# Cross-attention with image tokens: the products with the values, one step for both query tiles

## The chip, the cores and the metric

One core of a Trainium2 chip. The metric is device time in microseconds. The kernel before takes 710.52 us, the median of 3 runs (709.02 to 711.61).

## The reference

All in float32: x is 2 x 2048 x 640, the context 2 x 154 x 1024, of which the last 8 tokens are image tokens (4 "dummy", 4 for boxes). 20 heads of 32.

```python
q = split_heads(x @ w_q)
k, v = split_heads(text @ w_k), split_heads(text @ w_v)            # 146 text tokens
out_text = merge(softmax(q @ k.T / sqrt(32)) @ v)
k_ip, v_ip = split_heads(ip @ w_k_ip), split_heads(ip @ w_v_ip)    # 8 image tokens
out_ip = merge(softmax(q @ k_ip.T / sqrt(32) + mask_of_boxes) @ v_ip)
out = (out_text + out_ip) @ w_out + b_out + x
```

## The kernel before, in words

**Blocks.** The 4096 queries are done in 16 blocks of 256, each of two tiles of 128 (`qt` 0 and 1). Heads are taken in 5 groups `g` of 4. One loop iteration works on three blocks: the attention of block t - 1 ("back"), the query projection and first maxima of block t ("front"), and the transposed input of t + 1 ("next"). Four tables write down the order on each engine by hand: `STEPS` (TensorE), `ACT_STEPS` (ScalarE), `DVE_STEPS` (VectorE), `POOL_STEPS` (GpSimd); `SP_STEPS` holds the order of SyncE's DMAs.

**Steps.** X: transpose the input. Q g: project a group's queries in 15 matmuls (L1046); ScalarE copies the rounded part, VectorE writes the rest (L816). S g, qt, pair: scores of two heads (L1104); VectorE takes the maxima (L824, L825). AUX: the maxima, transposed, become rows of the stacked queries `q_stack`. ST g, u: transposed scores minus maxima; u = 0 and 1 are 128 text keys of two heads each (L1129), u = 2 the tail: 18 text keys and 8 image keys of all four heads at 32 rows for each head (L1134). ScalarE takes exp twice for u < 2, to 16 bits (`p_hi`) and in place (L676, L678), VectorE writes the difference `p_lo` (L852); for u = 2 ScalarE writes `p_tail`, 128 rows of float32 (L680). PV g, qt: the product with the values. AT: transpose the result; O: project it (L1046).

**PV before.** One step for each query tile, into one PSUM bank. First the tail, a float32 matmul over 128 rows and 264 columns, which the trace shows as two passes (L1150): 8 pieces of 33 columns, 4 heads' text part and 4 heads' image part with their denominators. Then 12 matmuls in 16 bits for the four heads' main keys (L1156, L1158, L1159). VectorE inverts the 8 denominators (L860) and multiplies them in (L865, L868) into `o_parts`; GpSimd adds three parts into `attn` (L530, L535).

**Banks.** X, Q, AUX, PV and O share three "general" PSUM banks in turn, S has two, ST has three. A step waits until the bank's user three places before has been read:

```python
    def user_before(self, gen):
        mine, theirs = users(self.stages), users(self.earlier)
        n = gen - GENERAL_BANKS
```

**Waits used below.** PV g waits for `exp_done` and `p_split` of its group. ST waits for `p_lo` three ST steps before. S waits for the maxima two S steps before (`s_freed`). AT waits for `att_done`. SyncE's step STK 0 rewrites `q_stack` for groups 0 to 2 of the next block: it waits for ST of those groups, the last of which is ST 2, 1, issues 12 copies and one of the mask, and S 0, 0, 0 waits for all of them (`stack_in`).

**Set-up.** The weights of keys and values are loaded in pieces; keys are copied into `k_stack` by 24 DMAs; the values are made in 8 units between the first steps (`V_PLACES`).

Of the kernel before, what the change touches and what calls it, by code (L numbers as in the profile page):

```python
# [31 lines left out]
F32 = mybir.dt.float32  # L32
# [3 lines left out]
ALU = mybir.AluOpType  # L36
# [3 lines left out]
P = 128  # L40
# [48 lines left out]
    (FRONT, "S", 2, 0, 0), (FRONT, "S", 2, 0, 1), (BACK, "O", 1, 0), (NEXT, "X", 2), (FRONT, "S", 2, 1, 0),  # L89
    (FRONT, "S", 2, 1, 1), (BACK, "O", 1, 1),  # L90
# [41 lines left out]
V_UNITS = [("ip", 0), ("ip", 1), ("text", 0), ("text", 1),  # L132
           ("main", 0, 0, 512), ("main", 0, 512, D), ("main", 1, 0, 512), ("main", 1, 512, D)]
V_TAILS = 4
V_BANKS = (5, 6, 7, 5, 6, 7, 5, 6)
V_PLACES = {
# [4 lines left out]
}  # L141
V_COPY_PLACES = {(0, "S", 0, 0, 0): (0, 1), (0, "S", 0, 0, 1): (2, 3), (1, "Q", 0): (4,), (1, "Q", 1): (5,), (1, "ST", 0, 2): (6, 7)}
V_SPLIT_PLACES = {(1, "S", 3, 0, 0): (4,), (1, "S", 3, 1, 0): (5,), (1, "S", 4, 0, 1): (6, 7)}
W_O_HIGH = {("Q", 0): (0, 1), ("Q", 1): (2, 3, 4)}
W_O_LOW = {("S", 3, 0, 1): (0, 1), ("S", 3, 1, 1): (2, 3), ("S", 4, 0, 0): (4,)}


GENERAL = {"X": 1, "Q": 1, "AUX": 1, "PV": 1, "O": 1}
# [17 lines left out]
def users(stages):  # L166

    return [s for s in STEPS if s[0] in stages and s[1] in GENERAL]

# [59 lines left out]
def attention_kernel(nc, x, ctx, boxes, wq, wk, wv, wk_ip, wv_ip, wo, b_out,  # L229
# [5 lines left out]
    with ExitStack() as stack:  # L235
# [20 lines left out]
        v_tail = [sb(f"v_tail{b}", [P, GROUPS, 8 * VW]) for b in range(BATCHES)]  # L256
# [29 lines left out]
        inv_den = sb("inv_den", [P, QT, 8])  # L286
# [8 lines left out]
        o_parts = sb("o_parts", [P, QT, 12, DH])  # L295
# [17 lines left out]
        product_2 = [general[i][:, 0:4 * VB].rearrange("p (e d) -> p e d", d=VB)[:, :, VW:VB] for i in range(GENERAL_BANKS)]  # L313
# [7 lines left out]
        s_wv, s_wv_ip, s_wq, s_wo, s_wk_ip = sem("wv_in"), sem("wv_ip_in"), sem("wq_in"), sem("wo_in"), sem("wk_ip_in")  # L321
# [6 lines left out]
        s_kst = [sem(f"k_stack{b}_in") for b in range(BATCHES)]  # L328
        s_vp, s_vc, s_ktail = sem("v_product"), sem("v_copied"), sem("k_tail_ready")
# [11 lines left out]
        norm_first = sem("first_part_normalised")  # L341
# [22 lines left out]
        def split_turn(n):  # L364

            return n - V_TAILS

# [3 lines left out]
        def keys_to_stack(queue, b, parts):  # L371

            for row, src in parts:
                for j in range(4):
                    queue.dma_start(k_stack[b][row:row + DH, j:HEADS:4, :].bitcast(F32),
                                    src[DH * j:DH * (j + 1), :, b, :].bitcast(F32)).then_inc(s_kst[b], 16)
# [13 lines left out]
        def _(sp):  # L390
# [300 lines left out]
        def _(dve):  # L691
# [111 lines left out]
            def body(it):  # L803
# [4 lines left out]
                for stage, kind, args, gen, sc in it.steps(DVE_STEPS):  # L808
# [437 lines left out]
```

## Time and profile before

| | |
|---|---|
| median of 3 runs | 710.52 us |
| profiled execution | 708.68 us |
| its span | 706.9 us |
| TensorE busy | 676.1 us, 96% |
| VectorE busy | 534.9 us, 76% |
| ScalarE busy | 290.4 us, 41% |
| GpSimd busy | 209.2 us, 30% |
| TensorE's mean granted clock | 0.995 of full speed |

The span goes from the first to the last instruction; 1.78 us lie around it. Blocks in the middle repeat every 38.4 us. Matmul records overlap: one starts before the one ahead has drained, so a matmul's cost in a stream is the distance between starts, and the chain of waits shows just that. On VectorE too the next instruction starts somewhat before the end that is shown.

### The profile page before, as it was taken

The numbers are of one execution on the slowest core, as the hardware profiler recorded it, in microseconds if no ns is written. First come the engines' busy times: TensorE is split into PE (matmuls) and PEld (weight loads), VectorE is DVE, ScalarE is ACT, GpSimd is POOL, SyncE is SP. The second block draws the span as 40 slices with busy tenths as digits, with TensorE's granted clock in tenths as the row PEclk, the third lists the DMA queues.
The fourth block names the chain that finished last, engine by engine and source line by source line (L and its number), as shares of the span: only waits on it lengthen the run. The fifth ranks groups of instructions, "written<-read, shape, count | busy, mean of one in ns | idle before, by whom it ended". The sixth has DMA issues, their size and how long they took to land.

```text
span 706.9 us, 19241 instructions
## 1 busy us (share of the span) xinstructions
PE 676.1 (96%) x6570; PEld 623.6 (88%) x6570; DVE 534.9 (76%) x1689; ACT 290.4 (41%) x636; POOL 209.2 (30%) x359
## 2 busy tenths in 40 slices
PE   6996988999999999999999999999999999999976
PEld 5794677989999999999998999999999989899866
DVE  4432678787878788887979787888879797879774
ACT  1232253351727263544526171726344352617161
POOL 5200006042423314150514242231515041423333
PEclk9998999999999999999999999999999999999999
DMA  9999326443526253534444352625354443434220
GB/s 295 379 278 210 93 36 139 131 106 86 146 71 177 68 157 93 132 97 130 102 118 118 90 154 69 177 73 150 89 136 100 129 103 110 122 89 124 68 76 38
DMA packets 74208, 89.40 MB, mean 126 GB/s; under 512 B 9440, under 2 KB 58080, under 8 KB 74156
## 3 DMA queue, kind: packets, MB, share of 16 engines
q1 hardware_dynamic: 70800, 86.48, 46.0%
q10 hardware_dynamic: 3372, 2.45, 1.8%
q8 instruction: 22, 0.36, 0.2%
q14 instruction: 14, 0.11, 0.1%
HBM read 39.21 MB, written 10.62 MB: 70 GB/s over the span
## 4 chain that ended last, share of the span: by engine, by line
PE 84%; DMA 6%; SPq 5%; DVE 4%; issue 1%; ACT 0%; POOL 0%; DVEq 0%
PE psum L1046 38%; PE psum L1104 10%; PE psum L1150 9%; PE psum L1134 5%; PE psum L1129 5%; SPq L384 3%; PE psum L1158 3%; DMA q_stack<-mask_scratch 3%; PE psum L1006 3%; DMA wo_raw<-in_L_xattn_w_k_ip 2%; PE psum L1159 2%; PE psum L918 2%; PE psum L1173 2%; PE psum L980 2%; PE psum L1156 1%
## 5 line engine op out<-in xcount | busy, mean ns | idle before, releaser
L530 POOL TENSOR_TENSOR attn<-o_parts 128x128 f32<-128x128 f32 x160 | 73.3, 458 | 421.9 <-DVE o_parts L865 387.3
L824 DVE TENSOR_REDUCE neg_max<-psum 128x2 f32<-128x292 f32 x320 | 144.8, 453 | 58.7 <-PE psum L1104 58.1
L1046 PE MATMUL psum<-wo_both,at_hi 128*128 128x320 f32 x640 | 153.2, 313 | 0.0
L1104 PE MATMUL psum<-k_stack,q_stack 104*128 104x154 f32 x640 | 114.5, 288 | 8.7 <-DMA q_stack<-mask_scratch 6.6
L1046 PE MATMUL psum<-xt_hi,wq_hi 128*128 128x256 f32 x400 | 114.1, 285 | 0.1
L1046 PE MATMUL psum<-xt_hi,wq_lo 128*128 128x256 f32 x400 | 111.1, 278 | 0.0
L1046 PE MATMUL psum<-xt_lo,wq_hi 128*128 128x256 f32 x400 | 111.1, 278 | 0.0
L852 DVE TENSOR_TENSOR p_lo<-psum,p_hi 128x512 f16<-128x512 f32 x160 | 107.9, 682 | 2.5 <-ACT psum L678 2.5
L1046 PEld LDWEIGHTS psum<-wo_both,at_hi 128*128 128x128 f32 x640 | 109.6, 188 | 0.0
L676 ACT ACTIVATE p_hi<-psum 128x512 f16<-128x512 f32 x160 | 95.2, 595 | 31.0 <-PE psum L1129 31.0
L1104 PEld LDWEIGHTS psum<-k_stack,q_stack 104*128 104x128 f32 x640 | 90.0, 191 | 19.6 <-issue 10.2
L1150 PE MATMUL psum<-v_tail,p_tail 128*128 128x264 f32 x320 | 101.5, 398 | 2.9 <-DVE o_parts L868 1.6
L1046 PE MATMUL psum<-wo_both,at_lo 128*128 128x320 f32 x320 | 98.7, 308 | 0.0
L678 ACT ACTIVATE psum<-psum 128x512 f32<-128x512 f32 x160 | 96.6, 603 | 0.0
L663 ACT ACTIVATE q_hi<-psum 128x256 fp32r<-128x256 f32 x80 | 30.9, 387 | 133.0 <-PE psum L1046 130.5
L535 POOL TENSOR_TENSOR attn<-attn,o_parts 128x128 f32<-128x128 f32 x160 | 73.2, 457 | 12.6
L1046 PEld LDWEIGHTS psum<-xt_hi,wq_hi 128*128 128x128 f32 x400 | 75.4, 189 | 0.3 <-DVE q_lo L816 0.3
L1046 PEld LDWEIGHTS psum<-xt_hi,wq_lo 128*128 128x128 f32 x400 | 75.4, 188 | 0.1
L1046 PEld LDWEIGHTS psum<-xt_lo,wq_hi 128*128 128x128 f32 x400 | 75.2, 188 | 0.0
L865 DVE TENSOR_TENSOR o_parts<-psum,inv_den 128x256 f32<-128x256 f32 x160 | 67.9, 424 | 8.6 <-POOL attn L535 3.1
L1158 PEld LDWEIGHTS psum<-v_main,p_hi 128*128 128x128 f16 x640 | 56.4, 96 | 20.1
L1159 PE MATMUL psum<-v_main,p_lo 128*128 128x65 bf16 x640 | 71.6, 191 | 0.0
(95 smaller groups left out, 1249.1 us busy)
## 6 DMA issues: line engine op xcount, KB each, us to landing
q_stack<-q_hi SPq DMA_DIRECT2D x128, 96.0 KB
x_in<-in_x SPq DMA_DIRECT2D x16, 640.0 KB, 5.4
x_res<-in_x SPq DMA_DIRECT2D x16, 640.0 KB, 5.4
out<-out_sb SPq DMA_DIRECT2D x32, 320.0 KB
q_stack<-q_hi SPq DMA_DIRECT2D x128, 64.0 KB
q_stack<-q_lo SPq DMA_DIRECT2D x60, 96.0 KB
q_stack<-q_lo SPq DMA_DIRECT2D x60, 64.0 KB
q_stack<-aux_a SPq DMA_DIRECT2D x48, 64.0 KB, 2.4
```

The lines of the kernel that those rows point to most:

```text
L530: nc.gpsimd.tensor_tensor(cols, o_parts[:, qt, 0:4, :], o_parts[:, qt, 4:8, :], ALU.add).then_inc(att_half, 1)
L535: nc.gpsimd.tensor_tensor(cols, cols, o_parts[:, qt, 8:12, :], ALU.add).then_inc(att_done, 1)
L676: nc.scalar.activation(p_hi[:, -g % P_SLOTS, 2 * u:2 * u + 2, :].rearrange("p h q -> p (h q)"), src[:], ACT.Exp)
L678: nc.scalar.activation(src[:], src[:], ACT.Exp).then_inc(exp_done, 1)
L824: nc.vector.tensor_reduce(dst[:, :, 0], src[:, :, 0:TEXT], AX_X, ALU.max, negate=True)
L852: nc.vector.tensor_tensor(p_lo[:, -g % P_SLOTS, 2 * u:2 * u + 2, :], scores_t[ST_TURN[(g, u)] % ST_BANKS][:].rearrange("p (h q) -> p h q", ...
L865: nc.vector.tensor_tensor(o_parts[:, qt, 0:8, :], product_1[it.general_bank(gen)][:, :, 0:DH], inv_den[:, qt, :].unsqueeze(2).to_broadcast ...
L1046: last = nc.tensor.matmul(ps, l(c), r(c), start=(i == 0), stop=(i == len(terms) - 1))
L1104: last = nc.tensor.matmul(scores[sc % 2][:, i * CTX:(i + 1) * CTX], q_stack[0:ROW_MAX, h, P * qt:P * (qt + 1)], k_stack[batch][0:ROW_MAX, ...
L1150: nc.tensor.matmul(product_1[it.general_bank(gen)][:, 0:8, :], p_tail[:, -g % P_SLOTS, queries], v_tail[batch][:, g, :].rearrange("p (e d) ...
L1158: nc.tensor.matmul(bank_a[:, VB * j:VB * (j + 1)], hi, values[:, 0:VB], start=False, stop=False)
L1159: last = nc.tensor.matmul(bank_a[:, VB * j:VB * (j + 1)], lo, values[:, 0:VB], start=False, stop=(j == 3))
```

## The change

PV becomes one step a group, for both query tiles. Its tail product is cut by rows: rows 0 to 63 (heads 0 and 1 of the group) go into one general bank, rows 64 to 127 (heads 2 and 3) into the next, 132 columns each, the two query tiles side by side in a bank. The main products follow, first those of bank r = 0, then of r = 1. VectorE normalises each bank by itself, GpSimd adds both query tiles in one instruction. PV 4, 1, which stood after AT 0, 1, goes with PV 4, 0. Waits are made to fit.

```diff
-    (BACK, "ST", 1, 0), (FRONT, "Q", 2), (BACK, "AUX", 1), (BACK, "ST", 2, 2), (BACK, "ST", 1, 1), (BACK, "PV", 0, 0),
-    (BACK, "ST", 2, 0), (BACK, "ST", 2, 1), (BACK, "PV", 0, 1), (FRONT, "Q", 3), (BACK, "ST", 3, 0),
-    (BACK, "PV", 1, 0), (BACK, "ST", 3, 2), (BACK, "ST", 3, 1), (BACK, "PV", 1, 1), (BACK, "PV", 2, 0),
-    (BACK, "PV", 2, 1), (BACK, "ST", 4, 0), (BACK, "ST", 4, 1), (BACK, "PV", 3, 0), (BACK, "PV", 3, 1),
-    (BACK, "ST", 4, 2), (FRONT, "Q", 4), (BACK, "PV", 4, 0), (FRONT, "S", 0, 0, 0), (BACK, "AT", 0, 0),
-    (FRONT, "S", 0, 0, 1), (NEXT, "X", 0), (FRONT, "S", 0, 1, 0), (FRONT, "S", 0, 1, 1), (BACK, "AT", 0, 1),
-    (BACK, "PV", 4, 1), (FRONT, "S", 1, 0, 0), (BACK, "AT", 1, 0), (NEXT, "X", 1), (FRONT, "S", 1, 0, 1),
-    (BACK, "O", 0, 0), (BACK, "AT", 1, 1), (FRONT, "S", 1, 1, 0), (FRONT, "S", 1, 1, 1), (BACK, "O", 0, 1),
...
+    (BACK, "ST", 1, 0), (FRONT, "Q", 2), (BACK, "AUX", 1), (BACK, "ST", 2, 2), (BACK, "ST", 1, 1), (BACK, "PV", 0),
+    (BACK, "ST", 2, 0), (BACK, "ST", 2, 1), (FRONT, "Q", 3), (BACK, "ST", 3, 0), (BACK, "PV", 1), (BACK, "ST", 3, 2),
+    (BACK, "ST", 3, 1), (BACK, "PV", 2), (BACK, "ST", 4, 0), (BACK, "ST", 4, 1), (BACK, "PV", 3), (BACK, "ST", 4, 2),
+    (FRONT, "Q", 4), (BACK, "PV", 4), (FRONT, "S", 0, 0, 0), (BACK, "AT", 0, 0), (FRONT, "S", 0, 0, 1),
+    (NEXT, "X", 0), (FRONT, "S", 0, 1, 0), (FRONT, "S", 0, 1, 1), (BACK, "AT", 0, 1), (FRONT, "S", 1, 0, 0),
+    (BACK, "AT", 1, 0), (NEXT, "X", 1), (FRONT, "S", 1, 0, 1), (BACK, "O", 0, 0), (BACK, "AT", 1, 1),
...
 DVE_STEPS = [
...
+    (BACK, "ST", 1, 0), (FRONT, "Q", 2), (BACK, "ST", 1, 1), (BACK, "PV", 0), (BACK, "ST", 2, 0), (BACK, "ST", 2, 1),
+    (FRONT, "Q", 3), (BACK, "PV", 1), (BACK, "ST", 3, 0), (BACK, "ST", 3, 1), (BACK, "PV", 2), (BACK, "ST", 4, 0),
+    (BACK, "ST", 4, 1), (BACK, "PV", 3), (FRONT, "Q", 4), (BACK, "PV", 4), (FRONT, "S", 0, 0, 0),
+    (FRONT, "S", 0, 0, 1), (BACK, "AT", 0, 0), (NEXT, "X", 0), (FRONT, "S", 0, 1, 0), (FRONT, "S", 0, 1, 1),
+    (BACK, "AT", 0, 1), (FRONT, "S", 1, 0, 0), (BACK, "AT", 1, 0), (FRONT, "S", 1, 0, 1), (NEXT, "X", 1),
...
 SP_STEPS = [
-    (BACK, "AUX", 0), (BACK, "LAST"), (NEXT, "XIN"), (BACK, "XRES"), (BACK, "AUX", 1), (FRONT, "STK", 0), (FRONT, "STK", 1),
-    (BACK, "STORE"),
+    (NEXT, "XIN"), (BACK, "AUX", 0), (BACK, "LAST"), (BACK, "XRES"), (BACK, "AUX", 1), (FRONT, "STK", 0),
+    (FRONT, "STK", 1), (BACK, "STORE"),
...
-GENERAL = {"X": 1, "Q": 1, "AUX": 1, "PV": 1, "O": 1}
+GENERAL = {"X": 1, "Q": 1, "AUX": 1, "PV": 2, "O": 1}
...
+                        tiles = [it.general_bank(gen + r) for r in range(2)]
+                        for r in range(2):
+                            free_general(it, gen + r)
+                        for qt in range(QT):
+                            queries = slice(P * qt, P * (qt + 1))
+                            for r in range(2):
+
+                                rows = slice(64 * r, 64 * (r + 1))
+                                nc.tensor.matmul(product_1[tiles[r]][:, 4 * qt:4 * qt + 4, :], p_tail[rows, -g % P_SLOTS, queries],
+                                                 v_tail[batch][rows, g, :].rearrange("p (e d) -> p e d", d=VW),
+                                                 start=(qt == 0), stop=False)
+                        for r in range(2):
+                            for qt in range(QT):
...
+                            last.then_inc(pv_ready, 1)
...
+                        for r in range(2):
+                            part, first = o_parts[:, g % 2, r, :, :], product_1[it.general_bank(gen + r)]
+
+                            dve.wait_ge(pv_ready, 2 * n + r + 1)
+                            nc.vector.reciprocal(inv_den[:, r, :], first[:, :, DH]).then_inc(recip_done, 1)
+                            dve.wait_ge(recip_done, 2 * n + r + 1)
+                            nc.vector.tensor_tensor(part[:, 0:8, :], first[:, :, 0:DH],
+                                                    inv_den[:, r, :].unsqueeze(2).to_broadcast([P, 8, DH]), ALU.mult)
...
-                        pe.wait_ge(att_done, t * 10 - 10 + (7 if u == 0 else 9) + qt)
+                        pe.wait_ge(att_done, t * 5 - 5 + (4 if u == 0 else 5))
```

The set-up changes too. Of the three pieces of the values' weights (L407), SyncE loads the second and third only after the first STK 0. Of the 8 key copies that SyncE issued ahead of STK 0, 4 go to GpSimd, as do 8 that ScalarE issued for the second batch. The main value units are cut at 256 columns instead of 512, and two of them stand ahead of the text tails, which so move behind the first scores.

```diff
-                    keys_to_stack(sp, 0, K_PARTS[:2])
+                    keys_to_stack(sp, 0, K_PARTS[:1], s_kst[0])
...
+                        if not it.back and n == 0:
+                            load_values(1)
+                            load_values(2)
...
+            keys_to_stack(nc.gpsimd, 0, K_PARTS[1:2], s_kst_own[0])
+            pool.wait_ge(q_freed, GROUPS)
+            keys_to_stack(nc.gpsimd, 1, K_PARTS[:2], s_kst_own[1])
```

## Rows read from the trace of the kernel before

**Rows 1.** The page, part 1: busy time, share of the span, instructions.

```profile
PE 676.1 (96%) x6570; PEld 623.6 (88%) x6570; DVE 534.9 (76%) x1689; ACT 290.4 (41%) x636; POOL 209.2 (30%) x359
```

**Rows 2.** Windows: stretch, then busy time of each engine, granted clock, DMA share, GB/s.

```profile
313.68:352.07 38.39, 38.34 (x381) 36.29 (x380) 31.70 (x103) 16.94 (x39) 12.02 (x21) 1.00 0.43 115
331.00:348.00 17.00, 17.00 (x209) 15.55 (x207) 15.20 (x46) 11.74 (x26) 7.27 (x16) 1.00 0.52 135
```

**Rows 3.** Chain of waits, 331 to 353 us: start, length, who.

```profile
333.93 0.45 PE psum L1150 x2
...
334.72 0.55 PE psum L1129 x4
...
338.89 0.55 PE psum L1134 x4
...
340.48 0.53 PE psum L1150 x2
...
344.97 1.77 PE psum L1046 x15
...
347.56 0.22 DVE inv_den L860
...
348.80 0.09 DVE neg_max L825
...
350.74 0.26 PE psum L1104 x2
...
352.07 1.07 PE psum L1046 x7
```

**Rows 4.** Groups by line: busy us, mean ns | idle before, releaser.

```profile
L1150 PE MATMUL psum<-v_tail,p_tail 128*128 128x264 f32 x320 | 101.5, 398 | 2.9 <-DVE o_parts L868 1.6 <-ACT p_tail L680 0.9 <-DVE p_lo L852 0.4
...
L1150 PEld LDWEIGHTS psum<-v_tail,p_tail 128*128 128x128 f32 x320 | 49.1, 191 | 3.3 <-DVE o_parts L868 1.7 <-ACT p_tail L680 1.0 <-issue 0.6
...
L1012 PE MATMUL psum<-w_kv,rest_t 128*26 128x160 f32 x128 | 5.0, 300 | 1.4 <-issue 1.4
...
L530 POOL TENSOR_TENSOR attn<-o_parts 128x128 f32<-128x128 f32 x160 | 73.3, 458 | 421.9 <-DVE o_parts L865 387.3 <-DMA bias<-in_L_xattn_b_out 34.6
```

**Rows 5.** Chain of waits, 136 to 162 us.

```profile
137.18 0.41 PE psum L1104 x4
...
152.20 3.29 DMA q_stack<-mask_scratch
```

**Rows 6.** VectorE's timeline, 314 to 353 us: start, length, line, tiles.

```profile
334.19 0.40 DVE L816 TENSOR_TENSOR q_lo<-psum,q_hi 128x256 fp32r<-128x256 f32 x1
...
341.30 0.68 DVE L852 TENSOR_TENSOR p_lo<-psum,p_hi 128x512 f16<-128x512 f32 x1
341.89 0.20 DVE L860 RECIPROCAL inv_den<-psum 128x8 f32<-128x8 f32 x1
...
342.66 0.20 DVE L860 RECIPROCAL inv_den<-psum 128x8 f32<-128x8 f32 x1
...
349.25 0.68 DVE L876 TENSOR_TENSOR at_lo<-psum,at_hi 128x512 fp32r<-128x512 f32 x1
349.84 0.45 DVE L824 TENSOR_REDUCE neg_max<-psum 128x2 f32<-128x292 f32 x1
...
350.29 0.68 DVE L754 TENSOR_TENSOR xt_lo<-psum,xt_hi 128x512 fp32r<-128x512 f32 x1
```

**Rows 7.** ScalarE's timeline, 334 to 336 us.

```profile
334.01 0.59 ACT L676 ACTIVATE p_hi<-psum 128x512 f16<-128x512 f32 x1
334.49 0.61 ACT L678 ACTIVATE psum<-psum 128x512 f32<-128x512 f32 x1
```

**Rows 8.** SyncE's DMA issues, 314 to 362 us.

```profile
335.30 2.52 SPq L384 DMA_DIRECT2D q_stack<-q_hi  x4
...
343.18 0.34 SPq L458 DMA_DIRECT2D q_stack<-mask_scratch  x1
```

**Rows 9.** Chain of waits, 0 to 128 us: the first scores wait for this.

```profile
51.36 11.06 DMA q_stack<-mask_scratch
```

More of the change, by code:

```diff
@@ L166, in users @@
 def users(stages):
-    return [s for s in STEPS if s[0] in stages and s[1] in GENERAL]
+    return [(*s, r) if GENERAL[s[1]] > 1 else s
+            for s in STEPS if s[0] in stages and s[1] in GENERAL for r in range(GENERAL[s[1]])]
 class Iteration:
@@ L255, in attention_kernel @@
         v_main = [sb(f"v_main{b}", [P, HEADS, VALUES], BF16) for b in range(BATCHES)]
-        v_tail = [sb(f"v_tail{b}", [P, GROUPS, 8 * VW]) for b in range(BATCHES)]
+        v_tail = [sb(f"v_tail{b}", [P, GROUPS, 4 * VW]) for b in range(BATCHES)]
         max_cols = [80, 16 * len(SET_B)]
@@ L294, in attention_kernel @@
             ctx_t = sb("ctx_t", [P, CC, BATCHES * TEXT], where=setup)
-        o_parts = sb("o_parts", [P, QT, 12, DH])
+        o_parts = sb("o_parts", [P, 2, 2, 12, DH])
         attn = sb("attn", [P, QT, D])
@@ L312, in attention_kernel @@
                      for i in range(GENERAL_BANKS)]
-        product_2 = [general[i][:, 0:4 * VB].rearrange("p (e d) -> p e d", d=VB)[:, :, VW:VB] for i in range(GENERAL_BANKS)]
+        product_2 = [psum[:, 512 * i:512 * i + 8 * VB].rearrange("p (q e d) -> p q e d", q=QT, d=VB)[:, :, 0:2, VW:VB]
+                     for i in range(GENERAL_BANKS)]
         s_ident, s_ctx, s_ctx_rest = sem("ident_in"), [sem(f"ctx{b}_in") for b in range(BATCHES)], sem("ctx_rest_in")
@@ L328, in attention_kernel @@
         s_kst = [sem(f"k_stack{b}_in") for b in range(BATCHES)]
+        s_kst_own = [sem(f"k_stack{b}_in_by_gpsimd") for b in range(BATCHES)]
         s_vp, s_vc, s_ktail = sem("v_product"), sem("v_copied"), sem("k_tail_ready")
@@ L645, in body @@
                             w_high(GROUPS + n)
-                    if not it.back and (kind, *args) == ("S", 0, 0, 1):
-                        act.wait_ge(stored, 16 * BATCHES)
-                        keys_to_stack(act, 1, K_PARTS[:2])
                     if kind == "X":
@@ L992, in make_values @@
                     if (n, first) == (2, 0):
-                        pe.wait_ge(s_wv, 16 * len(W_V_PIECES))
-                    if first == 0 and 3 <= n < 7:
-                        pe.wait_ge(s_vc, n - 2)
-                    if (n, first) == (7, 0):
-                        pe.wait_ge(s_vsplit, V_PARTS * split_turn(4) + 1)
+                        pe.wait_ge(s_wv[0], 16)
+                    if (n, first) == (4, 0):
+                        pe.wait_ge(s_wv[1], 16)
+                        pe.wait_ge(s_wv[2], 16)
+                    before = [m for m in range(n) if V_BANKS[m] == V_BANKS[n]]
+                    if first == 0 and before:
+                        if before[-1] in V_MAIN:
+                            pe.wait_ge(s_vsplit, V_PARTS * split_turn(before[-1]) + 1)
+                        else:
+                            pe.wait_ge(s_vc, before[-1] + 1)
                     ps = v_bank(n)
@@ L1161, in body @@
-                        last.then_inc(pv_ready, 1)
+                        g, = args
+                        if isinstance(t, int) and t == 1 and g == 0:
+                            pe.wait_ge(s_vc, 5)
+                            pe.wait_ge(s_vsplit, 3 * V_PARTS)
+                        pe.wait_ge(exp_done, t * ST_ALL - ST_ALL + 1 + max(ST_TURN[(g, u)] for u in range(3)))
+                        pe.wait_ge(p_split, t * 10 - 10 + 2 * g + 2)
+                        tiles = [it.general_bank(gen + r) for r in range(2)]
@@ new lines, in body @@
+                        for r in range(2):
+                            for qt in range(QT):
+                                queries = slice(P * qt, P * (qt + 1))
+                                for i in range(2):
+                                    j = 2 * r + i
+                                    at = VB * (4 * qt + i)
+                                    values, ps = v_main[batch][:, 4 * g + j, :], general[tiles[r]]
+                                    lo, hi = (p[:, -g % P_SLOTS, j, queries] for p in (p_lo, p_hi))
+                                    nc.tensor.matmul(ps[:, at + VW:at + VB], hi, values[:, VB:VALUES], start=False, stop=False)
+                                    nc.tensor.matmul(ps[:, at:at + VB], hi, values[:, 0:VB], start=False, stop=False)
+                                    last = nc.tensor.matmul(ps[:, at:at + VB], lo, values[:, 0:VB],
+                                                            start=False, stop=((qt, i) == (QT - 1, 1)))
+                            last.then_inc(pv_ready, 1)
```

158 lines of the change are left out of this document (71 added, 87 removed), and 9 rows, old and new, of the table V_PLACES.

## The prediction

> **What bounds the kernel now.** The page comes first: TensorE is busy for 96% of the span, VectorE for 76% [rows 1]. That alone would say that each microsecond taken from TensorE is gained, so the windows come next, one for a block and one for its PV stretch. A block in the middle takes 38.39 us; TensorE is busy throughout, VectorE for 31.70. But from 331 to 348 us, where ST and PV stand, VectorE has 15.20 us of work in 17.00 [rows 2]. The share of 76% is an average over two unlike halves, and the change takes time from TensorE in the half where VectorE is nearly full. The chain of waits shows how near: PV 4, 0 ends at 347.54, then the chain goes over VectorE (normalisation, then maxima) and comes back to TensorE only at 348.89, where S 0, 1, 0 needs a score bank [rows 3]. The reader is to see that VectorE already ends a wait once a block.
>
> **What TensorE saves.** In the chain a tail product costs 0.45 us behind an ST step and 0.53 behind another PV [rows 3]; there are seven of the first and three of the second in a block: 3.15 + 1.59 = 4.74 us. The 12 matmuls behind each take 0.34 (333.93 + 0.45 to 334.72), and their number stays. The new tail has four products of 64 rows and 132 columns a group. A pass of 264 columns takes 0.45 / 2 = 0.22, one of 132 so 0.11. No row shows two halves by rows. The bounds: if the halves run side by side, weight loads too, four passes, 0.44, and the start that PV behind PV shows, 0.53 - 0.45 = 0.08: 0.52. If nothing overlaps, eight passes, 0.88, and 0.08: 0.96. The nearest row is that of four tiles by columns, L1012: 128 records take 5.0 us, 0.039 each, where a pass of 160 columns alone would take 0.22 x 160 / 264 = 0.13 [rows 4]. Tiles do run side by side, so I take 0.55. Gain: 4.74 - 5 x 0.55 = 2.0 us a block. What could spoil it is the weights: S, with 154 columns, takes 0.41 / 4 = 0.10 a matmul [rows 5], more than its columns need (0.55 / 4 = 0.14 for 256, so 0.08), thus a load costs about 0.10, and eight one after the other 0.8. That is a rival below.
>
> The Trainium skill speaks against the change here: "TensorE: Matmul & The Clock Gate", section "LDWEIGHTS (loading the stationary operand)", says that a load takes as long for 32 rows as for 128, since the columns count, and "TensorEngine Tiling (Array Packing)", section "Key Properties", that a change of the tiling mode drains the engine, but also that tiles load and multiply independently. By the first with loads in line the tail would stay near 0.9 and the gain be nil; by the last it would be what I take. No run here shows which holds for rows.
>
> **What the new order makes wait.** VectorE's work per block stays: a bank's normalisation costs 0.77 (341.89 to 342.66) as before, ten of them; p_lo 0.59, AT 0.59, maxima 0.45 [rows 6], X, of AT's shape, 0.59. What changes is which bank is free when. I go through one block in the chain's times, with the new orders. ScalarE needs 1.10 from the start of p_hi to the end of the second exp [rows 7].
>
> 1. PV 0 takes two general banks at once. The second is that of Q 2, which VectorE frees at 334.19 + 0.40 = 334.59 [rows 6]. TensorE is there at 333.93 [rows 3]; before, only PV 0, 1 needed that bank, after two ST steps. Stall 0.70. Behind it stand ST 2, 0 and 2, 1, and behind them ScalarE and SyncE's STK 0.
> 2. PV 0: 334.63 to 335.86 (0.55 + 2 x 0.34). VectorE, now told to do ST 1, 1 first, idles until its exp ends at 335.10 and does it to 335.75; banks 0 and 1 to 337.3.
> 3. ST 2, 0 and 2, 1 end at 336.41, Q 3 (1.77) 338.18, ST 3, 0 338.42, PV 1 339.65. VectorE, waiting for the exps, does p_lo of group 2 to 338.9, Q 3 to 339.3, PV 1 from 339.33 (bank 0 ready) to 340.89, ST 3, 0 to 341.5, ST 3, 1 (exp ends 341.6) to 342.24.
> 4. ST 3, 2 (0.55) and 3, 1 end at 340.44, PV 2 341.67, ST 4, 0 and 4, 1 342.22. PV 3 needs the first bank of PV 2, which VectorE gets to after ST 3, 1: 342.24 + 0.78 = 343.02. Stall 0.84.
> 5. PV 3 ends at 344.29, ST 4, 2 344.85, Q 4 346.62, PV 4 347.87. VectorE is busy to 346.56, waits for Q 4, and normalises PV 4 from 347.55 to 349.11.
> 6. Then maxima of S 0, 0, 0 and 0, 0, 1, AT, X, maxima of S 0, 1, 0: 349.11 + 0.45 + 0.45 + 0.59 + 0.59 + 0.45 = 351.64. S 1, 0, 0 needs that last bank. Before, PV 4, 1 stood in front of S 1, 0, 0 and its normalisation behind the maxima, so that S 1, 0, 0 started at 350.74 [rows 3]. From there to O 0, 0 TensorE takes 352.07 - 350.74 = 1.33, now too: O 0, 0 starts at 351.68 + 1.33 = 353.0.
>
> Before it started at 352.07. From O 0, 0 on to the next PV 0 nothing is changed and VectorE has its idle time, so the block takes 0.94 us more: 2.0 saved, some 2.9 more in stalls. After each stall a weight load stands open, 0.08; two of the stalls are new, so I say 1.1 us a block.
>
> GpSimd's adds go from 128 to 256 elements; one of 128 takes 458 ns [rows 4], two of 256 at most 4 x 0.46 = 1.8 us, so PV 4 is in `attn` by 351.0, and AT 0, 1 behind it lies before S 1, 0, 0 is free (351.68): nothing. STK 0 costs nothing either, but just so: SyncE starts at 335.30, right after ST 2, 1, and issues the mask's copy at 343.18, 7.9 later [rows 8]; such a copy landed 3.29 after its issue [rows 5]. ST 2, 1 now ends at 336.41, S 0, 0, 0 can start at 336.41 + 7.9 + 3.3 + 0.1 = 347.7, and TensorE comes at 347.87. XIN ahead of AUX 0 on SyncE is cheap: its buffer is free before, and both issue long before ST.
>
> **Set-up and end.** The first scores wait for the mask's copy, issued at 51.36 and 11.06 us under way [rows 9], behind all other transfers. With fewer copies and two weight pieces less ahead of it I give it 5 us back; the text tails (L1012, 5.0 us [rows 4]), which filled that wait, then stand in TensorE's way later. Net -1, between -5 and +3. In the last block, where only "back" runs, PV 4 with both tiles stands before AT 0, 1: +1.
>
> **The sum**, against the profiled execution: 708.7 + 15 x 1.1 + 1 - 1 = 725. The median of before is 1.8 above that execution (0.3%), so I forecast 726 for the median.
>
> **Rivals.**
> - *Weight loads in line* (20%). The halves share one way for weights, the tail costs up to 0.95. The same steps with 0.95 give: PV 2's first bank free at 343.8, PV 3 to 345.5, PV 4 normalised at 350.67, 1.56 later, thus 2.65 a block: 708.7 + 15 x 2.65 + 2 = 750. For it: loads of 0.10. Against: four column tiles at 0.039 a record.
> - *Faster: VectorE's waits for exps close up* (18%). In my steps VectorE idles 1.8 us between 334.59 and 349.11, mostly waiting for ScalarE. If it finds work there, PV 4 is normalised by 348.0 and TensorE's 2.0 us come through until STK 0 holds it: S 0, 0, 0 at 347.73, O 0, 0 at 347.73 + (352.07 - 347.54 - 0.79 of PV 4, 1) = 351.5, 0.6 a block less: 708.7 - 15 x 0.6 - 2 = 698. It decides where PV 4's second bank is normalised less than 14.3 us after TensorE reached PV 0, and not 15.2. Against: the order is fixed, and each exp follows an ST that itself stands behind PV.
> - *No change* (7%): both effects meet, within 0.3% (2.1 us), which is about what a measurement of this kernel can tell.
> - My forecast (55%): 713 to 738 by itself, from the stalls being 0.7 us a block smaller or larger and the set-up's 4.
>
> Faster has 0.18, same 0.07, slower 0.75. The range reaches from 700, near the faster case, to 752, past the loads in line; outside lies some 15%.
>
> **What would show it.** Right: the PV stretch's tail at about 0.55 a group in the chain; TensorE's L1150 waiting on VectorE (q_lo L816 at PV 0, o_parts at PV 3) 15 times each; S 1, 0, 0 waiting on the maxima; the block at 39.5 us, with TensorE's busy time some 2 us lower and VectorE's 31.7 unchanged. Wrong: a block under 38.4 with VectorE full from PV 0 to O 0, 0; a tail of 0.9; or idle time at S 0, 0, 0 that the mask's copy ends.

## The result

The changed kernel takes 749.56 us, the median of 4 runs (744.59 to 751.46), beside 710.44 for the kernel before on the same chip: 1.0536 of its time, 95% interval [1.0505, 1.0566]. The forecast was 726. So the direction was right, and the loss, 39 us, is two and a half times the 15.5 that I gave it. The profiled execution's span is 748.2 us. Some executions of a kernel are over 1.5% above its fastest, at a lower granted clock: the medians here hold them, the ratios leave them out.

Part 1 of the page, after, beside [rows 1]:

```profile
span 748.2 us, 19481 instructions
...
PE 682.3 (91%) x6890; PEld 629.3 (84%) x6890; DVE 537.1 (72%) x1689; ACT 290.5 (39%) x636; POOL 185.7 (25%) x211
```

TensorE is busy for 6 us more in all, in a span that is 41 us longer. The windows show one block in the middle, from one O 0, 0 to the next, and its ST and PV stretch, as in [rows 2]:

```profile
245.47:286.37 40.90, 38.07 (x400) 35.87 (x400) 31.85 (x102) 16.95 (x39) 10.17 (x12) 1.00 0.44 108
262.92:280.00 17.08, 15.64 (x212) 14.23 (x210) 14.58 (x44) 11.74 (x26) 5.13 (x8) 1.00 0.50 119
```

A block takes 40.90 us where it took 38.39. From the first O 0, 0 to the fifteenth the two traces move apart by 34.9 us, 2.49 in each of 14 steps; 1.5 us lie ahead of the first and 4.9 behind the fifteenth, 41.3 in all. VectorE's work is 31.85, as said. TensorE idles for 2.83, and is busy for 0.27 less than before. I had forecast nearly the same idle time (2.9) and 2.0 less work. Where it idles, the groups by line tell (busy, mean ns | idle before, releaser):

```profile
L1131 PE MATMUL psum<-k_stack,q_stack 104*128 104x154 f32 x640 | 114.6, 290 | 21.8 <-DVE neg_max L842 15.3 <-DMA q_stack<-mask_scratch 6.4
...
L1181 PE MATMUL psum<-v_tail,p_tail 64*128 64x132 f32 x640 | 58.6, 302 | 24.0 <-DVE o_parts L887 12.6 <-DVE q_lo L833 11.1 <-ACT p_tail L697 0.3
```

L1181 is the tail product: 11.1 / 15 = 0.74 a block for q_lo at PV 0 (forecast 0.70), 12.6 / 15 = 0.84 for o_parts at PV 3 (forecast 0.84). L1131 is S, with 15.3 / 15 = 1.0 a block for the maxima, about half of it at S 0, 1, 0 and half at S 1, 0, 0. A fifth piece, 0.35 us at AT 0, 1 for GpSimd's `attn`, had been put at nothing; it costs nothing, since the chain does not pass through it. The chain of waits of the same block, beside [rows 3] (L1193 to L1195 are the main products, L1161 ST's tail, L1070 is Q and O):

```profile
266.16 0.41 DVE q_lo L833
...
266.62 0.72 PE psum L1181 x8
267.34 0.12 PE psum L1193
...
268.13 0.56 PE psum L1156 x4
268.69 1.77 PE psum L1070 x15
270.46 0.24 PE psum L1156 x2
270.70 0.65 PE psum L1181 x8
271.35 0.12 PE psum L1193
...
272.14 0.57 PE psum L1161 x4
...
275.65 0.72 PE psum L1181 x8
...
279.48 0.65 PE psum L1181 x8
...
284.34 0.37 DVE neg_max L841
...
284.85 0.45 PE psum L1131 x2
...
286.37 2.24 PE psum L1070 x15
```

Every wait of the forecast is there, at its place. What is not there is a PV of 0.55 + 0.68 = 1.23 us: they take 1.44 behind an ST step (270.70 to 272.14) and 1.51 after a wait (266.62 to 268.13). Less 0.68 for the 24 main products the tail costs 0.76 and 0.83. Laid on each other at ST 1, 1, in front of PV 0, the two traces are 68.03 us apart. With that shift the prediction's ledger reads:

| | forecast | measured | late by |
|---|---|---|---|
| PV 0 starts | 266.60 | 266.62 | 0.02 |
| PV 1 starts | 270.39 | 270.70 | 0.31 |
| PV 3 starts, behind o_parts | 275.03 | 275.65 | 0.62 |
| PV 4 starts | 278.61 | 279.48 | 0.87 |
| PV 4 normalised | 281.08 | 282.25 | 1.17 |
| S 1, 0, 0 starts, behind the maxima | 283.65 | 284.85 | 1.20 |
| O 0, 0 starts | 284.97 | 286.37 | 1.40 |

It gets later by 0.25 to 0.31 from row to row down to PV 4's normalisation (PV 1 to PV 3 is two PVs, and one step of 0.31). The 0.2 at the end is S 1, 0, 0 itself, whose two products take 0.45 right after a wait, where they took 0.26 [rows 3].

Why the tail costs that, the timeline of the weight loads shows, around PV 1:

```profile
270.63 0.53 PEld L1181 LDWEIGHTS psum<-v_tail,p_tail 64*128 64x128 f32 x8
271.28 0.10 PEld L1193 LDWEIGHTS psum<-v_main,p_hi 128*128 128x128 f16 x1
```

Eight loads from start to end in 0.53, where each by itself takes 0.19 [rows 4]. The single records start in pairs, 0.01 apart or less within a pair and 0.11 from pair to pair, which is the distance of single products in line: two run at a time, so the halves do overlap. But the first main product's load starts only at 271.28, 0.12 after the last tail load has ended, and in the chain the first main product then costs 0.12, where the others cost 0.02 to 0.04. On the way in, the first tail load (270.63) starts 0.21 after the product ahead of it (270.42), where products in line start 0.12 apart. By these rows TensorE seems to empty itself between products of 64 rows and of 128. "TensorEngine Tiling (Array Packing)" in the Trainium skill, section "Key Properties", says just that of a change of the tiling mode; I had named it in the prediction and put nothing into the sum for it.

### The profile page after: what moved, and what is told of

The parts are those of the page before. It is cut to its first block, busy times and chain, and to the rows that moved or that the text cites. A ratio compares the mean times of both kernels' runs of the same rounds, so it can differ in the third digit from the quotient of the medians.

```text
span 748.2 us, 19481 instructions
## 1 busy us (share of the span) xinstructions
PE 682.3 (91%) x6890; PEld 629.3 (84%) x6890; DVE 537.1 (72%) x1689; ACT 290.5 (39%) x636; POOL 185.7 (25%) x211
## 4 chain that ended last, share of the span: by engine, by line
PE 76%; DVE 11%; issue 6%; ACT 3%; DMA 2%; ACTq 1%; SPq 1%; POOL 0%; DVEq 0%; POOLq 0%
PE psum L1070 37%; PE psum L1131 8%; PE psum L1181 6%; PE psum L1161 5%; PE psum L1156 3%; PE psum L1000 3%; PE psum L1030 3%; PE psum L1194 2%; PE psum L1193 2%; PE psum L1195 2%; DVE neg_max L841 2%; DVE o_parts L887 2%; PE psum L938 2%; PE psum L1209 1%; ACT p_hi L693 1%
## 5 line engine op out<-in xcount | busy, mean ns | idle before, releaser
L549 POOL TENSOR_TENSOR attn<-o_parts 128x256 f32<-128x256 f32 x80 | 58.4, 730 | 491.3 <-DVE o_parts L887 460.4
L1070 PE MATMUL psum<-wo_both,at_hi 128*128 128x320 f32 x640 | 155.9, 317 | 0.0
L1131 PE MATMUL psum<-k_stack,q_stack 104*128 104x154 f32 x640 | 114.6, 290 | 21.8 <-DVE neg_max L842 15.3
L1131 PEld LDWEIGHTS psum<-k_stack,q_stack 104*128 104x128 f32 x640 | 91.5, 194 | 32.8 <-DVE neg_max L842 23.8
L1070 PE MATMUL psum<-xt_hi,wq_hi 128*128 128x256 f32 x400 | 113.4, 284 | 1.3 <-DVE q_lo L833 1.3
L1070 PEld LDWEIGHTS psum<-wo_both,at_hi 128*128 128x128 f32 x640 | 112.1, 192 | 0.3 <-issue 0.3
L1070 PE MATMUL psum<-xt_hi,wq_lo 128*128 128x256 f32 x400 | 111.7, 279 | 0.0
L1070 PE MATMUL psum<-xt_lo,wq_hi 128*128 128x256 f32 x400 | 111.7, 279 | 0.0
L1070 PE MATMUL psum<-wo_both,at_lo 128*128 128x320 f32 x320 | 100.0, 312 | 0.0
L1181 PE MATMUL psum<-v_tail,p_tail 64*128 64x132 f32 x640 | 58.6, 302 | 24.0 <-DVE o_parts L887 12.6
L906 DVE TENSOR_TENSOR out_sb<-psum,x_res 128x320 f32<-128x320 f32 x64 | 31.4, 491 | 64.0 <-PE psum L1070 64.0
L1070 PEld LDWEIGHTS psum<-xt_hi,wq_hi 128*128 128x128 f32 x400 | 75.2, 188 | 1.5 <-DVE q_lo L833 1.5
L1070 PEld LDWEIGHTS psum<-xt_hi,wq_lo 128*128 128x128 f32 x400 | 75.3, 188 | 0.1
L1070 PEld LDWEIGHTS psum<-xt_lo,wq_hi 128*128 128x128 f32 x400 | 75.0, 187 | 0.0
L1181 PEld LDWEIGHTS psum<-v_tail,p_tail 64*128 64x128 f32 x640 | 43.1, 189 | 37.1 <-DVE o_parts L887 11.2
L702 ACT ACTIVATE at_hi<-psum 128x512 fp32r<-128x512 f32 x64 | 28.0, 437 | 105.7 <-PE psum L1209 105.7
```

What stands on the lines that cost most here:

```text
L549: nc.gpsimd.tensor_tensor(cols, text, image, ALU.add).then_inc(att_half, 1)
L906: nc.vector.tensor_tensor(out_sb[:, qt, cols], bank_a[:, 0:HALF], x_res[:, qt, cols], ALU.add).then_inc(out_done, 1)
L1070: last = nc.tensor.matmul(ps, l(c), r(c), start=(i == 0), stop=(i == len(terms) - 1))
L1131: last = nc.tensor.matmul(scores[sc % 2][:, i * CTX:(i + 1) * CTX], q_stack[0:ROW_MAX, h, P * qt:P * (qt + 1)], k_stack[batch][0:ROW_MAX, ...
L1181: nc.tensor.matmul(product_1[tiles[r]][:, 4 * qt:4 * qt + 4, :], p_tail[rows, -g % P_SLOTS, queries], v_tail[batch][rows, g, :].rearrange( ...
```

## Experiments

Times are medians, with the ratio to the kernel before on the same chip. A block is undisturbed where O 0, 0 takes 2.24 us at both its ends (the last finding below says why that matters). Kernels with few such blocks are compared by a stretch of a block, from the start of an O 0, 0 that takes 2.24 to the start of S 1, 0, 0: 37.1 us before and 39.54 in the changed kernel, with 1.34 and 1.36 from there to the next O 0, 0.

**1. A ladder from the kernel before.** First the set-up alone: the changed kernel's set-up and XIN ahead of AUX 0, with PV of before.

> The kernel before with the changed set-up alone (order of the value units, the loads of the values' weights behind the first STK 0, key copies on GpSimd's queue, XIN first on SyncE); PV, its steps and orders are those of before. Theory: nearly all of the 39 us lies in the blocks, which are 2.5 us longer each, so this is 711 to 714 us, its blocks 38.4. Rival, the set-up costs much: 720 or more.

709.40, ratio 1.0003 [0.9967, 1.0039]. Blocks of 38.4 as before. Set-up and SyncE's order cost nothing.

Then the order: every PV g, 0 and PV g, 1 stand together, in the changed tables, each still with its own whole tail in its own bank, waiting for its own bank alone.

```diff
-    (BACK, "PV", 0, 0), (BACK, "ST", 2, 0), (BACK, "ST", 2, 1), (BACK, "PV", 0, 1), (FRONT, "Q", 3),
+    (BACK, "PV", 0, 0), (BACK, "PV", 0, 1), (BACK, "ST", 2, 0), (BACK, "ST", 2, 1), (FRONT, "Q", 3),
...
-    (BACK, "PV", 4, 0), (FRONT, "S", 0, 0, 0), (BACK, "AT", 0, 0),
+    (BACK, "PV", 4, 0), (BACK, "PV", 4, 1), (FRONT, "S", 0, 0, 0), (BACK, "AT", 0, 0),
```

> The changed set-up and the changed orders (PV g, 0 and g, 1 next to each other, PV 4, 1 ahead of AT, VectorE's new order), but each query tile keeps its whole tail in a bank of its own, and waits for that bank alone, in its turn. Theory: the stall at PV 0 is gone, since PV 0, 0 needs the bank of Q 1 and only PV 0, 1 that of Q 2; the end of the stretch (PV 4 normalised before the maxima) still costs about 1.1 us a block: 728 to 732. Rival, that the order alone makes the loss: 748 to 755. Rival, that only the cut by rows costs: 711 to 714.

741.12, ratio 1.0457 [1.0412, 1.0502]. That is between the theory and its rival. The stall at PV 0 is gone, as said; TensorE waits in one place, 1.07 us a block for the maxima at S 1, 0, 0. The stretch to S 1, 0, 0 takes 38.5 to 38.6, 1.5 more than before, or 22 of the 31 us. The rest is clock: ten of the first fifteen O 0, 0 take 2.7 to 3.6 us. So the order by itself costs most of what the change costs. Then both banks are waited for ahead of the first product:

```diff
+                        if qt == 0:
+                            free_general(it, gen + 1)
                         free_general(it, gen)
```

> As the run with the orders alone, but PV waits for both banks before its first product. What is left to the changed kernel is the cut by rows. Theory: both banks at once cost 1 to 1.5 us a block, and the cut by rows, which takes the two tails of a group from 0.98 to about 0.8 us, gives back 0.2 a group, so this is a little slower than the changed kernel: 750 to 756, PV 0 stalled 0.7 us a block. Rival, that the cut by rows makes the loss: 728 to 735, that is, as the run with waits in turn.

766.62, ratio 1.0823 [1.0777, 1.0869]: 25 us more, above the theory's range. The stretch takes 40.29, 1.7 more. From here the cut by rows leads to the changed kernel (with it GpSimd's adds over both tiles and a second set of `o_parts`) and gives back 17 us, 1.1 a block. In the stretch it is 0.75 a block; the rest of the 17 is clock, since five of the first fifteen O 0, 0 are slow here and two in the changed kernel. 2.0 had been forecast for the tail.

**2. The stall at PV 0.** ST 2, 0 and ST 2, 1 ahead of PV 0 in the changed kernel, where TensorE idles 0.74 for q_lo.

```diff
-(BACK, "ST", 1, 1), (BACK, "PV", 0), (BACK, "ST", 2, 0), (BACK, "ST", 2, 1), (FRONT, "Q", 3)
+(BACK, "ST", 1, 1), (BACK, "ST", 2, 0), (BACK, "ST", 2, 1), (BACK, "PV", 0), (FRONT, "Q", 3)
```

> The changed kernel with ST 2, 0 and ST 2, 1 moved ahead of PV 0 on TensorE. Theory: the 0.77 us in which PV 0 waits for the bank of Q 2 are filled with these 0.55 us, and ScalarE gets its exps of group 2 earlier: 0.6 to 0.9 us less a block, 736 to 741. Rival, that the loss sits in the later waits alone and takes this up: 747 to 750.

751.41, ratio 1.0581 [1.0513, 1.065]. The theory falls. An undisturbed block takes 40.80, 0.1 less: the stall of PV 0 is filled, but PV 4 is normalised as late as ever.

**3. The tail: overlap and change of mode.** The four products in the order "both tiles' rows 0 to 63, then both tiles' rows 64 to 127":

```diff
-                        for qt in range(QT):
-                            queries = slice(P * qt, P * (qt + 1))
-                            for r in range(2):
+                        for r in range(2):
+                            for qt in range(QT):
+                                queries = slice(P * qt, P * (qt + 1))
```

> The changed kernel with the four half products of a group in another order: both tiles' products of rows 0 to 63, then both of rows 64 to 127, so that neighbours mostly share their rows. In the changed kernel the products and their loads start in pairs 0.11 us apart, 0.44 us for the eight. Theory: a half of the rows 0 to 63 and one of the rows 64 to 127 run at the same time, and only neighbours can. Then at least half of the pairs come apart and the tail of a group takes 0.2 to 0.45 us longer, 1.0 to 2.2 us a block, 765 to 782 us. Rival: the halves overlap wherever they stand in the queue, or the pairs come from two copies of one product: nothing changes, 748 to 751 us.

747.36, ratio 1.0528 [1.0459, 1.0596]: no change, the rival holds, and the loads still start in pairs, 0.01 apart. The overlap doesn't need neighbours. Then the main products of a bank moved into the same loop, behind that bank's halves, so that 64 rows and 128 rows alternate twice a group:

> The same four half products, each bank's two now directly ahead of that bank's twelve main products, still behind the waits for both banks: TensorE changes between products of 64 rows and of all rows twice a group instead of once, with the same products and the same loads. Theory: the tail costs 0.25 us a group more than its products because TensorE empties itself at the change, in and out. Then this adds another 0.2 to 0.3 us a group to what the order of the halves costs by itself (the kernel with the halves in turn): 1.0 to 1.5 us a block, 15 to 23 us above that kernel. Rival: the change costs nothing, and the difference to my 0.55 us was the loads: within 3 us of that kernel, or below it, since the first bank is ready 0.2 us earlier.

795.94, ratio 1.1206 [1.1142, 1.1271], 46 us above the changed kernel, where 15 to 23 above the kernel just shown had been expected. The timeline of its loads, one of two parts of a group:

```profile
206.19 0.52 PEld L1180 LDWEIGHTS psum<-v_tail,p_tail 64*128 64x128 f32 x4
206.83 0.10 PEld L1191 LDWEIGHTS psum<-v_main,p_hi 128*128 128x128 f16 x1
```

Four loads of the same rows take as long as eight did in pairs. So this kernel lost the overlap and added a change of mode, and the two have to be told apart. Four products of all 128 rows in one part (both of the following leave each bank with the sums of all rows, so their result is another one) have neither overlap nor a change:

```diff
-p_tail[rows, -g % P_SLOTS, queries], v_tail[batch][rows, g, :]
+p_tail[:, -g % P_SLOTS, queries], v_tail[batch][:, g, :]
```

> The four half products of a group replaced by four products of all 128 rows with the same 132 columns into the same banks. The result then holds both halves' sums in each bank, so that the time alone means something. No product uses half of the rows any more. Theory: the cost of the change between the two kinds goes (0.25 us a group), but nothing runs in pairs (0.44 us more): 0.2 us a group more than now, the first of the eight loads again under the preceding products: block +0.5 to +1.3 us, 757 to 770 us. Rival: the change between the kinds costs more than the pairs give back, and this is faster than the changed kernel: 740 to 748 us.

768.43, ratio 1.0838 [1.0776, 1.09], as the theory said. And the same edit on the kernel with two changes:

> The kernel with two changes a group, with its half products replaced by products of all 128 rows in the same places (the result holds both halves' sums). Eight products and loads in line as there, in two parts of four, each ahead of its bank's main products, but TensorE never changes between products of 64 and of 128 rows. Theory: two changes a group cost 0.25 to 0.4 us each, so this is 35 to 60 us below that kernel's 796 us, and equal to the kernel with all eight products in one part (768 us) within 5 us. Rival: the split into two parts is what costs, and the change nothing: 790 to 800 us.

767.08, ratio 1.0822 [1.0781, 1.0863]. Equal to one part within 1.4 us: the split costs nothing. The 29 us up to 795.94 (27 by the two ratios, less than the 35 expected) are two changes of mode in each of 80 groups, 0.17 to 0.18 us each. That half products are slower in themselves is ruled out by the records: of the same rows they start 0.11 apart, as those of all rows do. The chains of the two show it (with all rows first, then with halves):

```profile
227.63 0.45 PE psum L1180 x4
228.08 0.02 PE psum L1191
...
228.42 0.53 PE psum L1180 x4
228.95 0.02 PE psum L1191
```

```profile
239.43 0.64 PE psum L1180 x4
240.07 0.12 PE psum L1191
...
240.52 0.64 PE psum L1180 x4
241.16 0.12 PE psum L1191
```

0.47 and 0.55 against 0.76 and 0.76: 0.25 on average in the chain. Where a PV follows a wait, it is 0.16. The stretch from O 0, 0 to S 1, 0, 0 takes 42.07 with halves and 40.40 with all rows, 0.17 for each of ten changes; PV 3's wait for o_parts, 0.46 a block, is gone in the slower kernel and hides a part. And all rows in one part cost 0.90 behind a step (193.89 to 194.79 in that kernel's chain), 1.00 at PV 2 and 1.17 behind a wait, against 0.76 and 0.83 with halves: 1.2 us a block, 0.24 a group, 19 us in 80 groups, and 18.9 was measured. Since the overlap by itself saves four of eight passes, 0.44, the change takes back 0.2.

**4. VectorE's share.** VectorE without its second multiplication (0.20 us, ten in a block); GpSimd adds the image part twice, the third part is left out of the result.

> The changed kernel without VectorE's second multiplication of each bank (0.20 us, ten in a block); GpSimd adds the image part twice instead, so that the third part of the result is left out. TensorE's work is the same. Theory: after the mis-sized tail the block is set by VectorE in its waits (PV 2's banks for PV 3, PV 4's normalisation ahead of the maxima of S 0,1,0): two banks behind PV 2 and two behind PV 4 each give back 0.2 us, so 0.6 to 1.2 us a block, 731 to 741 us. Rival: TensorE alone sets the block, with its own 0.25 us more a group: 747 to 751 us.

743.29, ratio 1.0471 [1.0413, 1.0529]. Between the two: undisturbed blocks take 40.25, 0.65 less, of 2.0 us less work. VectorE sets the pace through its two-bank waits, but only for a part.

The two maxima ahead of PV 4 instead of behind it:

> The changed kernel with the products and the maxima of S 0,0,0 and S 0,0,1 ahead of PV 4 on TensorE and VectorE, instead of behind it. In the changed kernel VectorE normalises PV 4's two banks until 282.25, then takes these two maxima (0.9 us), then those of S 0,1,0, for which S 1,0,0 waits (0.54 us). Theory: this chain sets the end of the block; VectorE takes the two maxima while TensorE does PV 4, whose end comes 0.55 us later, so 0.2 to 0.5 us a block are gained, 742 to 747 us. Rival: TensorE's 0.55 us ahead of PV 4 eat it, 748 to 753 us.

763.25, ratio 1.0757 [1.0682, 1.0831]. Neither theory: two waits that the prediction had priced at nothing took over, one of them "just so". Its chain:

```profile
573.84 3.23 DMA q_stack<-mask_scratch
577.07 0.12 issue
577.19 0.67 PE psum L1131 x4
577.86 0.65 PE psum L1181 x8
...
580.71 0.72 POOL attn L549
...
581.51 0.73 POOL attn L552
...
582.38 0.30 PE psum L1209
```

S 0, 0, 0, now in front, waits for the mask's copy, the last of STK 0, and PV 4 stands behind it; TensorE idles there for 0.6 us a block. A second term that had been put at nothing is larger: AT 0, 1 waits 1.8 us a block for GpSimd's two adds of PV 4, because two steps of TensorE's that stood between PV 4 and AT 0, 1 are gone from there. The stretch to S 1, 0, 0 takes 40.0, 0.5 more; the rest of the 14 us above the changed kernel is clock. Which of the two waits costs what was not tried.

**5. A tail shorter than the forecast's.** Both operands of the tail taken as bf16, the upper halves of the float32 numbers; the tail of the result is coarser.

```diff
-p_tail[rows, -g % P_SLOTS, queries]
+p_tail[rows, -g % P_SLOTS, queries].bitcast(BF16)[:, 1::2]
```

> The changed kernel with its tail products in bf16: both operands are the upper 16 bits of the f32 numbers, every second element, so that the result is that of a coarser tail. The halves of 64 rows, the order and all waits are as in the changed kernel. What is asked: how the block answers to a tail of the size that I had forecast. Theory: the tail now costs the change in and out (0.25 us) and little else, some 0.35 to 0.45 us a group instead of 0.76, the block follows five times that, 40.9 to 39.1 to 39.4 us, and the time is 720 to 730 us. Rival: VectorE sets the block, and a cheaper tail ends in longer waits: above 740 us.

740.23, ratio 1.0414 [1.0323, 1.0505]. The theory's time, 720 to 730 us, is missed. A tail now costs 0.41 behind a wait (0.29 in the chain and 0.12 for the first main product) and 0.34 behind a step, counted as the 0.83 and 0.76 were: 2.1 us a block less. Yet undisturbed blocks still take 39.4 to 39.6 (one from 410.98 to 450.59), 1.3 to 1.5 less, with TensorE busy for 36.14. Part of the miss is clock, ten slow O 0, 0.

> The same bf16 tail, but four products of all 128 rows in place of four of 64 (the result then holds both halves' sums in each bank). Now TensorE never changes between products of 64 and of 128 rows, and the products and loads are as short as the main ones beside them (0.03 to 0.06 us each). Theory: without the change nothing is left of the tail but four short products, 0.12 to 0.25 us a group: 0.15 to 0.3 us a group below the kernel with bf16 halves, so 10 to 20 us below it, 703 to 717 us. Rival: the change costs nothing where products are short: within 4 us of the kernel with bf16 halves.

739.81, ratio 1.0365 [1.0242, 1.0489]. The rival's time holds; undisturbed blocks take 39.4 and 39.5, after a first one of 40.2: the same. But this doesn't show that the change is free here. From its first product to the next step a PV takes 0.93, and 0.92 with halves, so four short products in line cost what the paired halves and their change cost; only the start comes 0.09 earlier, and TensorE waits in between anyway. What holds the block of the kernel with bf16 halves, its chain shows:

```profile
431.67 0.41 DVE q_lo L833
432.08 0.05 issue
432.13 0.29 PE psum L1181 x4
...
433.21 0.57 PE psum L1156 x4
...
433.79 0.59 SPq L390
...
442.32 3.23 DMA q_stack<-mask_scratch
445.56 0.12 issue
445.68 0.45 PE psum L1131 x2
```

PV 0's stall, then ST 2, 1, then SyncE's twelve copies and the mask. So ST 2 went ahead of PV 0 here too:

> The changed kernel with the bf16 tail and with ST 2, 0 and 2, 1 ahead of PV 0. Theory: in the kernel with bf16 halves the way that holds a block is SyncE's: PV 0 waits for Q 2's bank until 432.08 (0.9 us), ST 2, 1 ends after PV 0, and only then SyncE's copies begin (433.79), whose mask lands at 445.56, for S 0, 0, 0. With ST 2 in front SyncE starts 1.8 us earlier, the stall of PV 0 is filled, and a block takes 38.2 to 38.9 us instead of 39.6: 718 to 730 us. Rival: VectorE's own chain, which the same trace shows in other blocks, ends as late: 39.2 to 39.6, 734 to 744 us.

737.40, ratio 1.0409 [1.0345, 1.0473]. The rival's time holds. No block is undisturbed; the one whose O 0, 0 takes 2.24 needs 37.9 to S 1, 0, 0, where the kernel with bf16 halves needs 38.05 to 38.25. SyncE is out of the chain, and VectorE is in it: PV 3 waits for o_parts (ends 355.28), PV 4's normalisation ends at 357.75, S 1, 0, 0 starts at 360.35. Two ways end at nearly the same time, so taking away one gives 0.2 to 0.4 us.

Last, the bf16 tail in the kernel before, which frees and takes one bank at a time:

> The kernel before, with its tail products in bf16 (the upper 16 bits of both operands, a coarser tail) and nothing else changed. A tail product and its load then take 0.11 us or less instead of 0.45, ten in a block: TensorE has 3.4 us less to do in each block of 38.4. Theory: the kernel before is bound by TensorE, and by how much VectorE lies behind decides what of it is seen; in the changed kernel the block stopped falling at 39.5 us whatever the tail cost, because VectorE must free two banks at once; here it frees one at a time, so the block falls by 1.5 to 3 us and the time is 665 to 690 us. Rival: VectorE sets the block here too, at about 38 us, and the granted clock falls in the longer pauses: 700 to 712 us.

704.83, ratio 0.9921 [0.9893, 0.9950] over 8 runs: 0.8% below the kernel before, with a coarser tail; the theory's 665 to 690 is missed, and the rival's time is met. Most blocks take 37.1 to 37.5 instead of 38.4, four 38.9 to 40.4, each with a fall of the granted clock to half near its end. Of 3.4 us of TensorE's work a third comes through; then S 0, 0, 0 waits for the mask:

```profile
303.95 0.05 SPq L458
304.09 3.32 DMA q_stack<-mask_scratch
307.41 0.12 issue
307.53 0.45 PE psum L1104 x2
```

## Why the prediction was wrong in size

- **The step that failed** is the one that said "Tiles do run side by side, so I take 0.55. Gain: 4.74 - 5 x 0.55 = 2.0 us a block." The mechanism held (halves and their loads overlap), the term was mis-sized. Two tails behind a wait at 0.83 and three at 0.76 are 3.94, so the gain was 0.80. That is 1.2 us a block; with the 1.1 of the forecast 2.3, against 2.5 measured, or 18 of the 23.5 us that were missing. The bounds, 0.52 and 0.96, held it; the value was taken from the nearest row, L1012, whose 128 records follow each other in one mode. The mean over them says nothing of going in and out, and my 0.03 above the lower bound left no room for it. Experiment 3 puts the change of mode at 0.17 to 0.25 a group, 0.85 to 1.25 a block: most or all of the step's error. The trace of before had a hint just ahead of those records:

```profile
46.62 0.28 PE L1046 MATMUL psum<-xt_lo,wq_hi 128*128 128x256 f32 x1
46.83 4.55 PE L1012 MATMUL psum<-wo_raw,rest_t 128*26 128x160 f32 x128
```

From start to start these are 0.21 apart, where L1046's own follow at 0.11. The first L1012 also has a semaphore to wait for, so the row alone proves nothing, but it is the same 0.21 as on the way into the halves.

- **The waits** were right: PV 0 behind q_lo, PV 3 behind o_parts, S 1, 0, 0 behind the maxima, with 0.74 and 0.84 a block where 0.70 and 0.84 were said. That the order is what loses was right as well: the order with whole tails costs 31 us on its own, with both banks at once 57, and the cut by rows gives back 17. Of a block at full clock these are 1.5, 1.7 and 0.75 us; the rest is the clock, which the prediction did not consider.
- **How the error travels** was not thought through. Each PV's end releases VectorE, which releases the next PV, so the tail's error came back five times, one after another: 2 x 0.28 + 3 x 0.21 = 1.19, and the ledger is 1.17 late at PV 4's normalisation. That it doesn't travel for ever is experiment 5: of 2.1 us less tail a block gives 1.3 to 1.5. A tail of 0.55 would by the same count give 40.9 - 1.2 = 39.7, 1.3 a block; that is an estimate, no run had it.
- **Rival "weight loads in line", 750 us**: its time was met, its mechanism wasn't. The loads run in pairs, and the kernel in which they are really in line takes 768. A time alone would have confirmed the wrong story.
- **Rival "faster"**: VectorE's idle time for exps did not close up. In the PV stretch it is busy for 14.58 of 17.08 us, where it was 15.20 of 17.00, since each exp follows an ST that stands behind a PV.
- **Set-up, SyncE, GpSimd**: net nothing, as said (709.40). The mask's copy and GpSimd's adds cost nothing as long as S 0, 0, 0 stands behind PV 4; with both scores ahead of it they end waits, and the kernel is 14 us slower.
- **Left over**: of 2.5 us a block the tail's error and the forecast make 2.3; 0.2 is the slower S 1, 0, 0 behind its wait. Of the 4.9 us behind the fifteenth O 0, 0 (1 forecast) 1.7 is the last O 0, 0, which takes 3.86 us there instead of 2.19, with the clock falling; the rest is not taken apart. Of the first 1.5 us, 0 by the forecast (1.1 for one block less 1 for the set-up), 1.4 would be that block's own error; no run shows it apart.

## What to carry to other kernels

Cutting a short product by rows buys overlap and pays a change of mode each time: here 0.44 us gained a group and some 0.2 lost. At eight passes at a time between products of all rows half of the gain is lost; it should pay more where many such products stand together, which no run here tried. Where a step takes two buffers of three at once, write the ledger of who frees them before counting what the step saves: the order alone lost 31 us, both banks at once 25 more. Where two kernels are compared, look at blocks at full clock too: here a third of what one rung of the ladder seemed to give was the clock. And where the engine that is relieved and the one that follows release each other in turn, an error in one term comes back with each turn, until another wait takes over.

## What the runs showed of the hardware

The granted clock fell in most of these kernels, and not by how much they wait. In the kernel with bf16 halves, windows of 2 us ahead of and in O 0, 0 (the clock is the column after POOL's, 1.00 for 2.4 GHz, 0.50 for 1.2):

```profile
241.00:243.00 2.00, 1.90 (x18) 1.39 (x14) 1.93 (x9) 0.60 (x1) 1.06 (x2) 1.00 0.26 58
243.00:245.00 2.00, 1.19 (x5) 0.72 (x5) 2.00 (x7) 0.87 (x2) 1.92 (x3) 1.00 0.47 104
245.00:247.00 2.00, 1.92 (x12) 1.92 (x13) 1.33 (x7) 0.60 (x1) 1.95 (x1) 0.67 0.45 100
247.00:249.00 2.00, 2.00 (x9) 2.00 (x9) 1.53 (x4) 0.60 (x1) 0.00 (x0) 0.50 0.44 98
249.00:251.00 2.00, 2.00 (x17) 2.00 (x16) 0.52 (x2) 0.28 (x1) 0.00 (x0) 0.97 0.26 66
```

TensorE is busy for 1.19 of 2 us, and then its clock is halved for some 3 us, just where it has work again: X takes 0.85 instead of 0.44, O 0, 0 3.13 instead of 2.24, and the block 41.1 instead of 39.6. Of the first 15 O 0, 0 this met 10 there, 13 in the same kernel with ST 2 ahead of PV 0, and 10 in the kernel with only the order changed, but two in the changed kernel and none in the kernel before. The kernel with only the order changed waits for 1.07 us a block, in one piece ahead of S 1, 0, 0; the changed kernel for 2.8, in five pieces of at most 0.72. An equal pause doesn't always do it:

```profile
408.00:410.00 2.00, 1.11 (x8) 0.79 (x8) 2.00 (x8) 0.49 (x2) 2.00 (x2) 1.00 0.44 99
410.00:412.00 2.00, 2.00 (x18) 2.00 (x17) 1.48 (x6) 1.09 (x2) 1.33 (x1) 1.00 0.46 105
```

What decides was not tried. So in such kernels work taken from TensorE is paid back in part: with the bf16 halves some 10 x 1.4 = 14 us of the profiled execution's 745.4, which without them would have taken about 731 by this estimate.
